# Macaron block on one core: another order for the start, from the first load of x to the first expert tile

## The reference, cut to what matters

```python
x = x + 0.5 * ffn(layernorm(x))         # x: 4 batches x 1024 rows x 128
x = x + differential_attention(layernorm(x))
x = x + 0.5 * ffn(layernorm(x))

def ffn(tgt):                           # E = 8 experts, F = 512
    logits = einsum('bsd,ed->bse', tgt, Wr) + br
    top_v, top_i = top_k(logits, 2); top_w = softmax(top_v)
    h = relu(einsum('bsd,efd->bsef', tgt, W1) + b1)
    o = einsum('bsef,edf->bsed', h, W2) + b2
    return layer_norm(tgt + sum_over_e(o * router_w), gamma, beta)
```

## Time and profile before

| what | us |
|---|---|
| runs of the kernel before | 745.71, 749.78, 1200.47; median 749.78 |
| span of the profiled execution | 746.1 |
| lowest run beside that span | 745.71 |

### The profile page before, as it was taken

The page is one execution under the profiler, slowest core; times in us unless marked ns, Lnnn a source line. Parts: engine busy times, 40 slices in busy tenths (PEclk is TensorE's granted clock), DMA queues, the critical chain, the costliest instruction groups (busy, mean ns, idle before and its releaser), DMA issues.

```text
span 746.1 us, 16949 instructions
## 1 busy us (share of the span) xinstructions
PE 595.6 (80%) x4276; PEld 544.6 (73%) x4276; DVE 454.9 (61%) x1432; ACT 443.2 (59%) x1144; POOL 380.9 (51%) x475
## 2 busy tenths in 40 slices
PE   2626189999999879899898998969288479999955
PEld 1625079999998768787886897858187479999821
DVE  5527445654667788799688789655035236457636
ACT  4434056666665677678786866837054236786744
POOL 6345225541445277568324575835745645545633
PEclk9965579999999999999999999989679679999969
DMA  8412124443333111010000000212221222522042
GB/s 278 141 38 65 50 60 102 110 104 84 98 98 90 51 29 29 8 30 22 1 1 1 23 30 15 69 29 63 57 58 54 69 74 54 175 64 59 28 147 84
DMA packets 54253, 49.22 MB, mean 66 GB/s; under 512 B 9926, under 2 KB 45938, under 8 KB 53904
## 3 DMA queue, kind: packets, MB, share of 16 engines
q1 hardware_dynamic: 45312, 31.25, 15.0%
q0 software_dynamic: 8640, 16.87, 7.3%
q10 hardware_dynamic: 208, 0.02, 0.0%
HBM read 25.99 MB, written 23.02 MB: 66 GB/s over the span
## 4 chain that ended last, share of the span: by engine, by line
PE 51%; DVE 19%; issue 9%; another core or an unknown queue 7%; POOL 6%; ACT 6%; DMA 1%; ACTq 1%; DVEq 0%; POOLq 0%; SPq 0%
PE banks L953 17%; PE banks L963 16%; DVE nb L1607 4%; PE banks L946 3%; PE banks L1050 3%; DVE scratch L1614 2%; PE banks L885 2%; PE banks L887 2%; PE banks L886 2%; POOL zb L478 1%; POOL rs L455 1%; ACT scratch L639 1%; POOL rows L465 1%; DVE st_r L1217 1%
## 5 line engine op out<-in xcount | busy, mean ns | idle before, releaser
L963 PE MATMUL banks<-blocks,scratch 128*128 x1248 | 172.8, 283 | 24.6 <-issue 21.9
L963 PEld LDWEIGHTS banks<-blocks,scratch 128*128 128x128 f32 x1248 | 158.3, 199 | 26.8 <-issue 26.7
L953 PE MATMUL banks<-scratch 128*128 128x128 f32 x1248 | 173.4, 284 | 4.3 <-ACT scratch L639 3.0
L1357 DVE TENSOR_SCALAR scratch<-banks,blocks 128x128 f32<-128x128 f32 x312 | 95.2, 347 | 120.5 <-PE banks L953 68.8
L953 PEld LDWEIGHTS banks<-scratch 128*128 128x128 f32 x1248 | 157.9, 198 | 9.4 <-issue 9.2
L465 POOL DMA_INDIRECT rows<-rowbuf,slot x96 | 100.1, 1043 | 55.6 <-issue 48.6
L633 ACT ACTIVATE scratch<-banks 128x128 f32<-128x128 f32 x156 | 43.3, 277 | 136.0 <-PE banks L946 66.5
L489 POOL DMA_INDIRECT results<-scratch x78 | 79.2, 1015 | 77.0 <-DVE scratch L1365 45.4
L646 ACT ACTIVATE scratch<-banks,blocks 128x128 f32<-128x128 f32 x312 | 96.8, 366 | 14.3 <-remote 6.6
L721 ACT ACTIVATE scratch<-banks,nb 128x1024 f32<-128x1024 f32 x64 | 71.3, 1115 | 45.7 <-DVE nb L1607 45.1
L639 ACT ACTIVATE scratch<-blocks 128x512 f32 x156 | 97.5, 625 | 0.0
(11 more groups left out here) (210 smaller groups left out, 882.7 us busy)
## 6 DMA issues: line engine op xcount, KB each, us to landing
scratch<-rows SPq DMA_DIRECT2D x156, 64.5 KB
yrows<-scratch SPq DMA_DIRECT2D x78, 64.0 KB
rows<-padrows SPq DMA_DIRECT2D x34, 64.5 KB
x<-in_L_attn_x_dram SPq DMA_DIRECT2D x4, 512.0 KB, 5.6
scratch<-in_L_ffn_W_dram SPq DMA_DIRECT2D x1, 2048.0 KB, 19.3
rows<-rowbuf,slot POOLq DMA_INDIRECT x96
results<-scratch POOLq DMA_INDIRECT x78
zb<-results SPq DMA_DIRECT2D x1, 1024.0 KB
```

What stands on the lines that cost most here:

```text
L953: ins = pe.matmul(hT_at(T, c), staged(T, c), xT_of(T), start=True, stop=True)
L963: ins = pe.matmul(y_at(T), hT_of(T, c), blocks[:, W2_AT + c * D:][:, bass.ds(at, D)], start=(c == 0), stop=(c == FC - 1))
L1357: ins = dve.tensor_scalar(hT_of(T, c), hT_at(T, c), blocks[:, B1_AT + c:][:, bass.ds(at, 1)], 0.0, ALU.add, ALU.max)
```

## The change

SP loads batch 0 in two halves. DVE makes statistics by half, and 1/sqrt no longer comes from POOL: ACT takes the square root (`root`), DVE the reciprocal (`shifts`). PE turns identity matrices into an unused bank (`warm`) while it would wait: 30 ahead of the first rows, 20 ahead of the first prefix. The first half of batch 0 is turned and copied (by DVE) before the second half is ready. `place` makes the slots first and the weights afterwards, and batch 0's slots for the first choice are handed to POOL before those of the second. All of batch 1's routing on PE and ACT goes ahead of the weights' transposes, which are cut into two parts, one after each of the logits of batches 2 and 3, and ACT makes all 16 copies of them.

```diff
@@ SP
+            for h in range(2):
+                c = slice(h * TB * D // 2, (h + 1) * TB * D // 2)
+                sp.dma_start(x[:, c], x_v[0][:, c]).then_inc((x_first, x_loaded[0])[h], 16)
+            for b in range(1, BATCHES):
@@ POOL
-            for b in range(BATCHES):
-                rstd(b)
-            for b in range(GB):
-                scatter(0, b)
+            wait_apart(pool, (half_slots, 1), (rows_ready, 1))
+            scatter(0, 0, range(0, PAIRS, 2))
+            wait_apart(pool, (slots_ready, 1), (rows_copied, 1))
+            scatter(0, 0, range(1, PAIRS, 2))
+            scatter(0, 1)
@@ ACT
+                    act.wait_ge(wT_ps, 2 * g + 2)
+                    act.activation(blocks_v[:, g, W2_AT:W2_AT + F], bank(2 + g % 2), ACT.Copy).then_inc(w2_sb, 1)
+            def root(n, ready, tiles=range(TB)):
+                c = slice(tiles[0], tiles[-1] + 1)
+                act.wait_ge(*ready)
+                act.activation(rs[n % LN][:, c], mv[n % LN][:, c, 1], ACT.Sqrt, bias=eps[:, 0:1], scale=1.0).then_inc(root_ready, 1)
...
+            act.activation(ss[:, :], ones[:, 0:TB], ACT.Sqrt)
+            root(0, (half_stats, 1), halves_of(0))
+            first_rows(range(0, 2))
+            root(0, (ln_stats, 1), halves_of(1))
+            first_rows(range(2, 4)).then_inc(half_rows, 1)
+            make_rows(0, 0, 0, halves_of(1))
+            root(1, (ln_stats, 2))
+            copy_tgtT(0, 1)
+            make_rows(0, 1, 1)
+            root(2, (ln_stats, 3))
+            copy_rows(0, 0)
+            for i in range(2):
+                copy_tgtT(1, i)
+            root(3, (ln_stats, 4))
+            gap(0)
+            make_rows(0, 2, 2)
+            copy_rows(0, 1)
+            gap(1)
+            for i in range(2):
+                copy_tgtT(2, i)
+            weights(range(E // 2))
+            make_rows(0, 3, 3)
+            copy_rows(0, 2)
+            gap(2)
+            for i in range(2):
+                copy_tgtT(3, i)
+            weights(range(E // 2, E))
+            act.wait_ge(lam_ps, 1)
+            act.activation(lame[:, :], bank(3, 2 * D, 2 * D + 2), ACT.Exp).then_inc(lam_exp, 1)
+            copy_rows(0, 3)
+            gap(3)
@@ PE
+            def warm(n):
+                for _ in range(n):
+                    pe.transpose(bank(1, 0, P), ident[:, :], ident[:, :])
...
+            warm(30)
+            turn_rows(0, 0)
             router_weights()
+            turn_rows(0, 1)
             logits(0)
+            warm(20)
+            prefix(0)
+            for b in range(1, BATCHES):
+                for i in range(2):
+                    turn_rows(b, i)
+                logits(b)
+                if b > 1:
+                    weights(range((b - 2) * E // 2, (b - 1) * E // 2))
                 prefix(b)
...
@@ DVE
+            def shifts(n, roots, tiles=range(TB)):
+                dve.wait_ge(root_ready, roots)
+                steps.then(dve.reciprocal(rs[n % LN][:, c], rs[n % LN][:, c]))
+                return dve.scalar_tensor_tensor(nm[n % LN][:, c], mv[n % LN][:, c, 0], -1.0, rs[n % LN][:, c], ALU.mult, ALU.mult)
...
+            router_weights()
+            copy_first_turn()
...
+            row_numbers(0, 0)
+            read_logits(0)
+            at_once(choose(0))
+            placing = place_all(0)
...
+            shifts(2, 4).then_inc(ln_rstd, 1)
+            read_logits(1)
+            shifts(3, 5).then_inc(ln_rstd, 1)
+            at_once(placing)
+            at_once(choose(1))
+            at_once(place(1, 1))
+            at_once(table(0))
             for b in range(2, BATCHES):
+                read_logits(b)
+                at_once(choose(b))
+                at_once(place(b, b))
+                if b == 2:
                     small_weights()
+            minus_lambda()
+            dve.wait_ge(qkT_ps, 1)
+            dve.tensor_copy(qkwT[:, :], bank(4)).then_inc(qkT_sb, 1)
             at_once(table(1))
```

More of the change, by code:

```diff
@@ L428, in _ @@
             pool.memset(minus[:, :], -1.0)
+            pool.memset(eps[:, :], EPS)
             pool.memset(onesE[:, :], 1.0)
@@ L459, in scatter @@
             def scatter(p, b, pieces=range(2 * TB)):
-                if pieces[0] == 0:
+                if pieces[0] == 0 and p + b:
                     wait_apart(pool, (slots_ready, BATCHES * p + b + 1), (rows_copied, BATCHES * p + b + 1))
@@ L1195, in small_weights @@
                 dve.tensor_tensor(lamp[:, 1:2], lamv[:, 2:3], lamv[:, 3:4], ALU.mult).then_inc(lam_in, 1)
-            def weights(experts):
-                for g in experts:
-                    dve.wait_ge(wT_ps, 2 * g + 2)
-                    dve.tensor_copy(blocks_v[:, g, W2_AT:W2_AT + F], bank(2 + g % 2)).then_inc(w2_sb, 1)
             def minus_lambda():
@@ L1285, in place @@
                 yield
-                steps.then(dve.tensor_tensor(carry[:, :], carry[:, :], by_expert(run)[:, :, TB - 1], ALU.add))
                 sf = slotf[:, b * PAIRS:(b + 1) * PAIRS]
@@ L1291, in place @@
                     steps.then(dve.tensor_reduce(sv[:, :, k], by_tile(eq), AX_X, ALU.add))
+                    if a == 0 and k == 0:
+                        dve.tensor_copy(slot_v[:, b, :, 0], sv[:, :, 0]).then_inc(half_slots, 1)
                     yield
-                dve.tensor_copy(slot[:, b * PAIRS:(b + 1) * PAIRS], sf).then_inc(slots_ready, 1)
+                if a:
+                    dve.tensor_copy(slot[:, b * PAIRS:(b + 1) * PAIRS], sf).then_inc(slots_ready, 1)
+                else:
+                    dve.tensor_copy(slot_v[:, b, :, 1], sv[:, :, 1]).then_inc(slots_ready, 1)
+                steps.then(dve.tensor_tensor(carry[:, :], carry[:, :], by_expert(run)[:, :, TB - 1], ALU.add))
+                yield
+                dve.wait_ge(gap_exp, a + 1)
+                steps.then(dve.tensor_scalar(den[:, :], ex[:, :], 1.0, None, ALU.add))
+                w = wts[:, b * 2 * TB:(b + 1) * 2 * TB].rearrange("p (t k) -> p t k", k=2)
+                steps.then(dve.reciprocal(den[:, :], den[:, :]))
+                dve.tensor_copy(w[:, :, 0], den[:, :])
+                dve.tensor_tensor(w[:, :, 1], ex[:, :], den[:, :], ALU.mult)
                 yield
@@ L1662, in attention, with place_all @@
                 return n
-            for b in range(2):
-                dve.wait_ge(x_loaded[b], 16)
-                x_stats(b, b)
-            router_weights()
-            for b in range(2, BATCHES):
-                dve.wait_ge(x_loaded[b], 16)
-                x_stats(b, b)
-            for b in range(BATCHES):
-                route(0, b)
-                if b == 0:
-                    small_weights()
-                    weights(range(E))
-                if b == 1:
-                    at_once(table(0))
-                if b == 2:
-                    minus_lambda()
-                    dve.wait_ge(qkT_ps, 1)
-                    dve.tensor_copy(qkwT[:, :], bank(4)).then_inc(qkT_sb, 1)
+            def place_all(b):
+                placing = place(b, b)
+                for _ in range(5):
+                    next(placing)
+                return placing
```

127 lines of the change are left out of this document (63 added, 64 removed).

## The result

The changed kernel takes 755.67 us in the median (754.47 to 758.34), the kernel before, beside it, 745.71: a ratio of 1.015, interval 1.012 to 1.018. It is slower by 1.5%, where 742, a little faster, was forecast; the time lies just inside the upper end of the range of 725 to 757. Of the five executions of the kernel before one took 1200.47 us, and the ratio is of the others. The last experiments add something that no profile of one chip could show: on chip 10 both kernels take 678 us and agree within 0.3%, and the kernel before does so on chip 15 too.

A forecast was written before the change was run, and what follows sets the result against it. It took the start, 96.31 of 746.1 us, as what the change could move, with PE's posts late while POOL issues indirect DMAs; main loop 6.5 earlier gave 739.6, forecast as 742 for the median, range 725 to 757.

The forecast's parts named there:

- Up to the first piece: Start, from batch 0's load to POOL's first piece: first piece at 22.7 instead of 29.09, 6.4 us earlier.
- The clock's share: `warm` in the start: PE at its faster level, batch 0's logits in 1.9 us where they took 3.58.
- PE stays at the slower level: Rival, up to batch 0's logits: first piece at 25.2, all behind 2.5 later, 744.5; inside the forecast's range, no own chance.
- The second table load: ACT, before batch 1's first Exp at 25: a load of 1.28 us, costing the path 0 (bounds 0 and 1.3).
- One row of 32 pieces: POOL, batches 0 and 1: batch 1's slots ready at 36.9, pieces unbroken to 63.4 instead of 80.96.
- What is late next: PE's work for batches 2, 3 and weights: 2.4 us a post from 34.3, first main-loop product at 89.8, 6.5 earlier.
- the other side: Rival: batch 2's turn or logits held until POOL's row ends; start 108, 12 us later, 758 to 762; chance 0.12.
- The rest of the run: Both passes and attention behind the start: left as they are but for the order inside `place`, 0 us.
- The rival without a hold: Rival: PE's posts not delayed during POOL's back-to-back indirect DMAs; start at 73.4, 22.9 us earlier, 723 to 727; chance 0.22.

The follow-up runs named there:

- no_warm: The changed kernel without the 50 turned identities of `warm(30)` and `warm(20)`: 759.6 us, 1.0149 of the kernel before.
- pause_mid: The changed kernel with 24 small POOL multiplications, some 7 us, between batch 0's last piece and batch 1's first: 742.56 us, 0.9914 of the kernel before.
- weights_first: The changed kernel with all eight experts' weight turns and copies put back ahead of batch 1's logits: 754.05 us, 1.0064 of the kernel before.
- pause_one: The changed kernel with one small POOL multiplication behind each of the 32 pieces: 736.07 us, 0.9805 of the kernel before; on chip 10 684.51, 1.0089.
- before_one: The kernel before with one small POOL multiplication behind each of its 32 pieces: 737.49 us, 0.9824 of the unaltered kernel before.
- experts_first: The changed kernel with turns and copies of experts 0 to 3 ahead of batch 2's rows, 4 to 7 ahead of batch 3's: 677.51 us, 0.9994, on chip 15.
- pause_some: The changed kernel with one small POOL multiplication behind every second piece of batch 0 and every fourth of batch 1: 738.73 us, 0.9846 of the kernel before.
- after_again: The changed kernel unaltered, traced again on chip 10: 678.05 us, 0.9988 of the kernel before.

## Why the prediction was wrong, point by point

- **Up to the first piece** the sum came out, in part by luck: batch 0's logits in 1.95 us (12.60 to 14.55) for 13.9, read at 15.44 for 15.1, chosen at 18.93 + 0.22 for 18.8, first piece at 22.75 for 22.7. The first half of x is there at 3.94 for 4.2, but the second, for which the sum had no term, only at 8.88, though the undivided load of batch 0 was there at 4.69 in the kernel before. It sets the last rows (11.7 for 10.4) and the start of the logits. DVE was busy with other batches' statistics to 15.4 anyway, and the prefix took 0.76 for 1.2. The clock's share was needed (no_warm, above). The rival "PE stays at the slower level", priced at 25.2, came in five later traces, with logits of 3.41 to 3.58 us: their first pieces stand at 23.78 to 24.67. The 30 turned identities do not bring the faster level each time.
- **The second table load** lasts 1.28 us (25.26), as the forecast had it from the one load of the trace before. It stood on the chain (ACT's rows of batch 2 begin at 26.76 behind it), but what follows was then held 32 us; on chip 10 the chain goes through PE there, so the term of 0 for the path was right. No run shows the 2.7 us of the Trainium skill ("ScalarE: Activation LUTs", "Table sets: the hidden batching unit"): the activation behind the load begins at 26.55, 1.29 after the load began.
- **One row of 32 pieces**: slots ready at 34.60 for 36.9, last piece through at 63.21 for 63.4. Right.
- **"What is late next" failed, and with it the direction.** Its step was "from 34.3 on at 2.4 us a post": two turns and batch 2's logits at 41.5, eight posts of the experts at 60.7. The two turns were let go early, at 33.00 and 34.87, and from 35.5 to 66 nothing passed. I had taken a mean over seven waits of one row for a rate, though they were uneven (up to 6.38 beside some under 3), and one row further on the trace had a single post held 11.26 us. pause_mid shows batch 0's row without a trickle (ACT waits 10.46 us, to 2.9 behind its end), weights_first shows the trickle in a row of the same length. Its rate could not be carried from one order of work to another; what sets it, no run here shows.
- **The rival that came** is "the other side": "the hold takes batch 2's turn or logits", and by its own point of decision, batch 2's logits not read by 66 (66.38). Its price was too high, 108 for 100.87: it queued the second turn and the logits (5.3 us) behind 66.2, which PE had run by 39.1, and 4 of the 8 turns of experts 0 to 3 (3.4 us) had run too. Less these it gives 99.3, and ACT was let go at 67.84, 1.6 later than 66.2. I gave it 0.12 because seven posts had come through before; the last rows before the forecast, 11.26 us without one, were better evidence for a row twice as long.
- **The rest of the run** was counted as unchanged. It came out 2.0 us longer, and in pause_one 9.2 longer than before (659.0 for 649.8), 8.6 of them in the first pass (164.5 for 155.9). On chip 10, where nothing is held, the first pass is 1.8 us shorter after the change, not longer (152.2 for 154.0). What a held start does to the pass behind it, no run here takes apart.
- **The rival without a hold** forecast a start at 73.4. On chip 10 it is 74.81, by the steps it named: batch 3's logits at 58.67 for 56, prefix at 64.95 for 64, then 9.9 for 9.4. But it reckoned the gain against a start of 96.31 that was itself made of held posts. Without them the kernel before starts at 74.88, and the change is worth nothing: -0.1 us of start.

So the change removes a bound (the pieces, 17.7 us earlier) that was one only where posts are held (on chip 10 the kernel before waits for them too, but its M is ready only 0.7 us earlier), and where they are held it lengthens the row that holds them.

**The best version** depends on whether posts are held. Where they are, pause_one is faster than the kernel before beside it, 736.07 against 749.6, and before_one (737.49) is not told from it. Where they aren't, the changed kernel, the one before and experts_first are alike at 677.5 to 678.5, and pause_one is 6.5 us slower. There nothing tried here beats the kernel before.

## What to carry to other kernels

Before a wait in a trace is scheduled around, find out whether it is the kernel's: run the same program on a second chip, and reckon the gain against that. If engines stand before nameless waits while POOL issues indirect transfers back to back, don't make the row longer; put some 0.2 us of other work behind each transfer and see whether the waits go, then take it out where they don't appear. And a rate read off one row (so many us a post) is no forecast for another order of work: where one post was held to the end of a row, price the case in which the next one is too, however long the row becomes.

## What the runs showed of the hardware

- On chips 0 and 5 and in the first comparison a post of PE to ACT or DVE arrives up to 27.8 us late while POOL issues indirect transfers 0.30 us apart (expert 0's turn is through at 40.04, ACT goes on at 67.84; batch 2's logits 39.10 and 66.38). What a row still owes at its end arrives 0.7 to 5.0 us behind its last transfer (2.8 in the kernel before, 3.2 and 4.6 in the changed one, 0.7 in pause_mid's second row, 5.0 in no_warm). In the changed kernel's row the two longest waits are 25.0 and 32.4 us; over the whole run the kernel before is 66.1 us shorter where none is held (680.0 for 746.1). Chips 0 and 5 did it in every traced kernel with an unbroken row, chips 15 and 10 in none of six traces, three of them with such a row; the kernel before took 744.6 to 755.2 on the first two and 675.3 to 682.2 on the others. Every execution was traced, so whether one that isn't traced is held as well is open, as is whether it is the chip, its surroundings or the time.
- A gap of 0.5 us with a multiplication of 8 columns in it lets the posts through, behind every second piece as well as behind each in batch 0's row (no wait named remote in pause_some and pause_one there); behind every fourth, in batch 1's, it doesn't (6.67 and 5.08 us).
- DVE's and SP's own steps slow down too: in the changed kernel's row DVE's chain of small steps shows idle 0.66 and 1.13 us between two of its own at 39.78 and 41.17, where after_again has no gap, and SP's eight pad writes take 32.7 us (from 37.62) for 8.1 in after_again.
- Of a load cut in two, the second half can come later than the whole did: batch 0's 512 KB were there at 4.69 in one piece; in halves the first was there at 3.94 and the second at 8.88 (7.53 to 9.61 in sixteen traces).
- 30 turned identities ahead of batch 0's first turn gave the logits the faster level (1.95 us) in six of fifteen traces, the slower (3.41 to 3.58) in five and something between in four.
